# A decoder layer's MLP: up and gate products by seven block products in two passes, and the low parts of their weights on VectorE

## The reference

```python
qkv = _rms(x) @ w_qkv.T                     # x is LayerNorm(x) here
q, k, v = jnp.split(qkv, 3, axis=-1)
q, k = _rms(q), _rms(k)
w = jnp.exp(k)
y = sigmoid(q) * (cumsum(w * v) / (cumsum(w) + 1e-06))
u, g = jnp.split(y @ w_swiglu.T, 2, axis=-1)      # 2 x 2048 columns
x = x + u * silu(g) @ w_out.T
```

## Time and profile before

| | us |
|---|---|
| median of three runs | 1392.3 |
| the profiled execution: span | 1390.5 |
| TensorE busy | 1340.8 |
| VectorE busy | 819.9 |
| ScalarE busy | 606.6 |
| GpSimd busy | 513.0 |
| stage A, to the first `up` | 188.84 |
| the MLP, from there to the first transpose of the cross attention | 526.59 |

### The profile page before, as it was taken

One profiled execution on the slowest core, in us unless ns is written; L12 is line 12 of the kernel. 1 busy time (PEld: TensorE's weight loads), 2 busy tenths in 40 slices (PEclk: granted clock), 3 DMA queues, 4 the chain that ended last, 5 costly groups with the idle time before them and its releaser, 6 DMA issues.

```text
span 1390.5 us, 23678 instructions
## 1 busy us (share of the span) xinstructions
PE 1340.8 (96%) x8180; PEld 1068.0 (77%) x8180; DVE 819.9 (59%) x2085; ACT 606.6 (44%) x1135; POOL 513.0 (37%) x485
## 2 busy tenths in 40 slices
PE   8999999999999999999999999999988999999994
PEld 6788888888888888888886777777766877766762
DVE  5888865333333333333467787788786586666661
ACT  4444441111111111111126777777786324777772
POOL 4555542202020202020427554446453112655552
PEclk9999999999999999999999999999999999999997
DMA  6000002010110101010100000000011924566553
GB/s 257 1 0 0 0 30 107 0 46 5 42 38 8 45 0 45 0 46 1 49 12 17 21 21 21 21 5 17 6 47 46 374 81 159 92 106 105 95 98 46
DMA packets 20533, 73.41 MB, mean 53 GB/s; under 512 B 2320, under 2 KB 3344, under 8 KB 18000
## 3 DMA queue, kind: packets, MB, share of 16 engines
q1 hardware_dynamic: 10256, 46.93, 9.3%
q0 software_dynamic: 10176, 25.17, 9.2%
HBM read 52.95 MB, written 19.14 MB: 52 GB/s over the span
## 4 chain that ended last, share of the span: by engine, by line
PE 86%; DVE 6%; ACT 4%; issue 2%; DMA 1%; POOL 1%; POOLq 0%; DVEq 0%; SPq 0%; ACTq 0%
PE ps L782 21%; PE ps L784 21%; PE ps L783 21%; PE ps L1030 5%; PE ps L1215 5%; PE ps L1022 2%; DVE den L1641 2%; ACT cols L1434 2%; PE ps L1054 2%; PE ps L1122 2%; PE ps L1048 1%; ACT cols L1422 1%; PE ps L1185 1%; PE ps L1143 1%; PE ps L1019 1%
## 5 line engine op out<-in xcount | busy, mean ns | idle before, releaser
L782 PE MATMUL ps<-feat,wsplit 128*128 128x512 f32 (+1 forms) x672 | 247.1, 368 | 3.2 <-PE ps L784 2.1
L784 PE MATMUL ps<-feat,wsplit 128*128 128x512 f32 (+1 forms) x672 | 244.6, 364 | 0.0
L783 PE MATMUL ps<-feat,wsplit 128*128 128x512 f32 (+1 forms) x672 | 244.5, 364 | 0.0
L1291 ACT ACTIVATE sg<-ps 128x512 f32<-128x512 f32 x64 | 38.3, 598 | 369.1 <-PE ps L784 369.0
L1561 DVE TENSOR_TENSOR m_f<-ps,sg 128x512 f32<-128x512 f32 x64 | 44.2, 691 | 245.4 <-ACT sg L1291 245.4
L542 POOL CAST wsplit<-wraw 128x3072 fp32r<-128x3072 f32 x9 | 24.8, 2755 | 399.3 <-PEq L970 386.7
L1829 DVE CUSTOM_DVE_ANT_0 cols<-ps,msk 128x256 f32<-128x256 f32 (+1 forms) x512 | 146.2, 353 | 27.7 <-PE ps L1022 16.3
L782 PEld LDWEIGHTS ps<-feat,wsplit 128*128 128x128 f32 x672 | 126.7, 189 | 26.4 <-issue 6.6
L1422 ACT COPY cols<-ps 128x512 f32<-128x512 f32 x192 | 111.6, 581 | 77.7 <-PE ps L1030 77.7
L784 PEld LDWEIGHTS ps<-feat,wsplit 128*128 128x128 f32 x672 | 126.6, 188 | 19.9
L783 PEld LDWEIGHTS ps<-feat,wsplit 128*128 128x128 f32 x672 | 126.7, 189 | 19.7
(11 more groups left out here) (281 smaller groups left out, 3014.5 us busy)
## 6 DMA issues: line engine op xcount, KB each, us to landing
wraw<-weights SPq DMA_DIRECT2D x11, 1536.0 KB, 6.5
rawx<-weights SPq DMA_DIRECT2D x8, 1536.0 KB, 16.1
ctx_raw<-ctx_t SPq DMA_DIRECT2D x8, 512.0 KB, 4.6
h_rows<-hd POOLq DMA_DIRECT2D x16, 256.0 KB, 4.4
out<-acc SPq DMA_DIRECT2D x4, 1024.0 KB, 4.7
qkv_raw<-weights SPq DMA_DIRECT2D x6, 512.0 KB, 7.5
acc<-x SPq DMA_DIRECT2D x1, 3072.0 KB, 17.5
acc<-x SPq DMA_DIRECT2D x2, 512.0 KB, 7.0
```

The lines of the kernel that those rows point to most:

```text
L782: nc.tensor.matmul(out_, w_hi, m_hi, start=first, stop=False)
L783: nc.tensor.matmul(out_, w_lo, m_hi, start=False, stop=False)
L784: return nc.tensor.matmul(out_, w_hi, m_lo, start=False, stop=last)
```

## The change

Up and gate of a pair of token chunks are one product of a 2x2 block matrix of weights (rows: gate and up; columns: the two halves of K) by a 2x2 block matrix of y (the halves of K; two chunks of 512 tokens). The change makes it with seven block products in place of eight: sums of weight blocks (S1 to S4) and sums of y blocks (T1 to T4) are made first, and the seven products p1 to p7 are added up, in PSUM where one follows another in the same bank, and by copies (ScalarE) and additions (VectorE) elsewhere. A pass takes 1,024 tokens (batches 0 to 3, then 4 to 7) through all 8 groups, so there are 16 turns (`TURNS`), and all weights are loaded twice.

On TensorE, a product and its waits, `down`, and a turn:

```diff
+            def product(u, j, bank, w_op, y, y_op, first):
+                w = w_up[u % 2]
+                for k in range(HALF):
+                    out_ = ps[:, bank[j], :]
+                    w_hi, w_lo = w[:, j, 0, w_op, k, :], w[:, j, 1, w_op, k, :]
+                    y_hi, y_lo = y[:, y_op, 0, k, :], y[:, y_op, 1, k, :]
+                    nc.tensor.matmul(out_, w_hi, y_hi, start=first and k == 0, stop=False, skip_group_check=True)
+                    nc.tensor.matmul(out_, w_lo, y_hi, start=False, stop=False, skip_group_check=True)
+                    mm = nc.tensor.matmul(out_, w_hi, y_lo, start=False, stop=k == HALF - 1, skip_group_check=True)
+                return mm
...
+            def p1(u, j):
+                after(pe, mlp["silu2"], JB * (u - 1) + j + 1)
+                if u == 0 and j == 1:
+                    pe.wait_ge(a["w"], TILES)
+                pe.wait_ge(mlp["w_up"], JB * u + j + 1)
+                y_ready(u, 1)
+                product(u, j, BANK_X, A11, ya, B11, True).then_inc(mlp["P1"], 1)
...
+            def down(u, t):
+                chunk, o = t // 4, slice(t % 4 * P, (t % 4 + 1) * P)
+                pe.wait_ge(mlp["lo"], 2 * JB * u + JB * (chunk + 1))
+                pe.wait_ge(mlp["w_dn"], u + 1)
+                after(pe, mlp["acc"], PIECES * u + t - 1)
+                for j in range(JB):
+                    mm = three(pe, ps[:, BANK_D[t % 2], :], m_s[:, 0, j, chunk, o], m_s[:, 1, j, chunk, o],
+                               w_dn[u % 2][:, 0, j, :], w_dn[u % 2][:, 1, j, :], j == 0, j == JB - 1)
+                mm.then_inc(mlp["down"], 1)
...
+            for u in range(1, TURNS):
+                p1(u, 0)
+                p1(u, 1)
+                p2(u, 0)
+                p2(u, 1)
+                if u == 1:
+                    pe.wait_ge(a["y"], 2 * BATCH)
+                down(u - 1, 0)
+                p7(u, 0)
+                p7(u, 1)
+                down(u - 1, 1)
+                p6(u, 0)
+                p6(u, 1)
+                down(u - 1, 2)
+                down(u - 1, 3)
+                p5(u, 0)
+                p5(u, 1)
+                down(u - 1, 4)
+                p4(u, 0)
+                p4(u, 1)
+                down(u - 1, 5)
+                down(u - 1, 6)
+                p3(u, 0)
+                p3(u, 1)
+                down(u - 1, 7)
```

On VectorE, the weights' low parts (`low_plain`, `low_sums`), and where they and `first_rows` stand in a turn:

```diff
+            def low_of(v, j, ops, n):
+                dve.wait_ge(mlp["w_hi"], 4 * v + n)
+                to, raw = w_up[v % 2], w_up_raw[v % 2]
+                dve.wait_ge(mlp["ws"], v + 2)
+                return nc.vector.tensor_tensor(out=to[:, j, 1, ops, :, :].rearrange("p o k n -> p (o k n)"), in0=raw[:, j, 1, ops, :].rearrange("p o n -> p (o n)"),
+                                               in1=to[:, j, 0, ops, :, :].rearrange("p o k n -> p (o k n)"), op=ALU.subtract)
+            def low_plain(v):
+                for j in range(JB):
+                    low_of(v, j, slice(A11, A22 + 1), j + 1)
+            def low_sums(v, j):
+                low_of(v, j, slice(S1, S4 + 1), JB + j + 1).then_inc(mlp["w_up"], 1)
...
+            for u in range(1, TURNS):
+                gate_1(u, 0)
+                gate_1(u, 1)
+                sum_down(u - 1, 0)
...
+                if u + 1 == TURNS:
+                    first_rows()
+                sum_down(u - 1, 1)
...
+                sum_down(u - 1, 4)
+                up_1(u, 0)
+                up_1(u, 1)
+                hidden_1(u, 0)
+                hidden_1(u, 1)
+                sum_down(u - 1, 5)
+                if u + 1 < TURNS:
+                    low_plain(u + 1)
+                low(u, 0, 0)
+                low(u, 1, 0)
+                sum_down(u - 1, 6)
+                if u + 1 < TURNS:
+                    low_sums(u + 1, 0)
+                hidden_2(u, 0)
+                hidden_2(u, 1)
+                sum_down(u - 1, 7)
+                if u + 1 < TURNS:
+                    low_sums(u + 1, 1)
+                low(u, 0, 1)
```

On GpSimd, the sums of weights, the low part of the down weights, the second pass's sums of y, and (first lines) the first two of the ten pieces of y sums that stand behind the low parts of half batches (3,0) to (7,1) of stage A:

```diff
+                    if (b, tt) == (3, 0):
+                        y_sums(0, (T3, T1))
+                    if (b, tt) == (3, 1):
+                        y_sums(0, (T2, T4))
...
+            def weight_sums(to, of, a21, js):
+                s1 = own.mark(nc.gpsimd.tensor_tensor(out=to[:, js, 1, S1, :], in0=a21, in1=of(A22), op=ALU.add))
+                own.mark(nc.gpsimd.tensor_tensor(out=to[:, js, 1, S3, :], in0=of(A11), in1=a21, op=ALU.subtract))
+                own.wait(s1)
+                own.link(nc.gpsimd.tensor_tensor(out=to[:, js, 1, S2, :], in0=to[:, js, 1, S1, :], in1=of(A11), op=ALU.subtract))
+                nc.gpsimd.tensor_tensor(out=to[:, js, 1, S4, :], in0=of(A12), in1=to[:, js, 1, S2, :], op=ALU.subtract).then_inc(mlp["ws"], 1)
...
+            def split_dn(v):
+                pool.wait_ge(mlp["dn_hi"], v + 1)
+                nc.gpsimd.tensor_tensor(out=w_dn[v % 2][:, 1, :, :], in0=w_dn_raw[v % 2][:, 1, :, :], in1=w_dn[v % 2][:, 0, :, :], op=ALU.subtract).then_inc(mlp["w_dn"], 1)
...
+            def second_sums():
+                s_, n = a["T"], 2 * 4
+                pool.wait_ge(mlp["U2"], JB * MLP_GROUPS)
+                pool.wait_ge(a["y"], 2 * BATCH)
+                nc.gpsimd.tensor_tensor(out=y_whole(yt_raw, T3, 1), in0=y_chunk(1, 1), in1=y_chunk(1, 0), op=ALU.subtract).then_inc(s_, 1)
+                pool.wait_ge(s_, n + 1)
+                nc.gpsimd.tensor_tensor(out=y_whole(yt_raw, T2, 1), in0=y_whole(yt_raw, T3, 1), in1=y_chunk(0, 0), op=ALU.add).then_inc(s_, 1)
...
+            for u in range(TURNS):
+                if u + 1 < TURNS:
+                    split_up(u + 1)
+                split_dn(u)
+                if u + 1 == MLP_GROUPS:
+                    second_sums()
```

On ScalarE, the casts of the weights:

```diff
+            def up_hi(v):
+                act.wait_ge(raw_up, 32 * v)
+                for j in range(JB):
+                    nc.scalar.copy(w_up[v % 2][:, j, 0, A11:A22 + 1, :, :].rearrange("p o k n -> p (o k n)"),
+                                   w_up_raw[v % 2][:, j, 1, A11:A22 + 1, :].rearrange("p o n -> p (o n)")).then_inc(mlp["w_hi"], 1)
+                for j in range(JB):
+                    sums_hi(v, j, v + 2)
+            def dn_hi(v):
+                act.wait_ge(raw_dn, 16 * (v + 1))
+                nc.scalar.copy(w_dn[v % 2][:, 0, :, :], w_dn_raw[v % 2][:, 1, :, :]).then_inc(mlp["dn_hi"], 1)
```

More of the change, by code:

```diff
@@ L380, in decoder_layer @@
             w_hi="tiles of its hi", wv="tiles of w * v", wv_hi="tiles of its hi", split="tiles with w and w * v split",
-            w_hi_piece="pieces of w_qkv with hi", w_piece="pieces split", w2_hi="parts of the first MLP slot with hi", w2="parts split", shift="batches whose residual's scale and shift are made",
+            w_hi_piece="pieces of w_qkv with hi", w_piece="pieces split", shift="batches whose residual's scale and shift are made",
             w_sum="running sums of w, half batches", scan="those of w * v and exp(-q)^T too", wce="w's sums plus 1e-6",
-            den="denominators", rec="their reciprocals", y="outputs, half batches", yhi="their hi in feat", yT="their lo too",
+            den="denominators", rec="their reciprocals", y="outputs, half batches", yhi="operands made of them, their hi", yT="their lo too", T="sums of outputs", T_lo="the first pair's, split",
             pool="GpSimd's own small steps", dve="the vector engine's")
@@ L417, in decoder_layer @@
         mlp = signals(
-            "mlp_", up="up and gate in PSUM", silu="silu(gate)", m="silu(gate) * up", hi="its hi", lo="its lo",
-            down="sums in PSUM", acc="sums added to the residual")
+            "mlp_", P1="product 1 in PSUM", gate0="a copy of it", P2="product 2 in PSUM", P7="product 7 in PSUM", up0="a copy of it", gate1="first chunk's gate", silu1="its silu", U2="products 1 and 6", us="a copy of them",
+            U4="products 1, 6, 5 and 7", up2="second chunk's up", V="product 7 less product 4", up1="first chunk's up", X="second chunk's gate in PSUM", silu2="its silu",
+            m="silu(gate) * up", hi="their hi", lo="their lo", down="sums in PSUM", acc="sums added to the residual",
+            ws="slots with the weights' sums", w_hi="pieces of up weights with hi", w_up="hidden blocks with up weights split", dn_hi="slots with down weights' hi", w_dn="slots with down weights split")
         block = es.enter_context(nc.Block())
@@ L1003, in turned_unit @@
+            pe.wait_ge(mlp["silu2"], JB * TURNS)
+            for t in range(TPB):
+                turn_h(0, t, ps[:, 2 + t, :])
+            pe.wait_ge(slot_w, 1)
+            pe.wait_ge(c["ctx_s"], 1)
+            keys(ps[:, 0, :])
+            values(ps[:, 1, :])
+            for t in range(PIECES):
+                down(TURNS - 1, t)
+            pe.wait_ge(c["hT"], TPB)
+            for half in range(2):
+                queries(half, ps[:, 2 + half, :])
             def turned_unit(b, u):
```

873 lines of the change are left out of this document (522 added, 351 removed).

## The result

The changed kernel took 1438.1 us (median of 4 runs, 1435.7 to 1447.4) against 1392.2 before: a ratio of 1.034, with a 95% interval of 1.031 to 1.037. It is slower by 46 us, where 37 were forecast; the time lies in the stated range.

A forecast was written before the change was run, and what follows sets the result against it. TensorE was taken as the bound, busy 1340.8 of 1390.5 us, by matmul count and waits. Terms -43.5 + 31.9 + 9 + 25.3 + 4.1 + 13 - 3.0 = +36.8 gave 1429 us, range 1404 to 1454.

The forecast's parts named there:

- (a): TensorE in the MLP: 192 fewer matmuls at 0.2267 us each, -43.5 us.
- (b): Turn ends in the MLP: TensorE waits 2.28 us for VectorE's weight subtractions at 14 boundaries, +31.9 us.
- (c): Stage A: GpSimd's added pieces of y sums delay the scales and `ha`, +9 us, bounds 0 and 14.
- (d): First turn: waits of 13.2 us before and 8.7 us after it, 3.4 us for the clock, together +25.3 us.
- (e): Turn 7: GpSimd's y sums for the second pass hold two VectorE instructions, +4.1 us, bounds 0 and 6.
- (f): Turn 15: TensorE waits for a sum behind the first rows, which wait for their scale, +13 us.
- (g): MLP: the 3.0 us it lost before are replaced by the new waits, -3.0 us.
- Rival B: Turn ends: the weight subtractions are covered, VectorE being idle over 60% of the MLP; 1385 us, chance 0.11.
- Rival C: Stage A: GpSimd's new pieces don't reach TensorE, the start waits 7 us less; 1413 us, chance 0.14.
- rival E: Every turn: GpSimd's 2.41 us subtraction holds VectorE behind p4, 14 times, 34 us; 1463 us, chance 0.04.
- Rival D: Turn boundaries: two close waits cost a clock drop of 1.7 us at each of 14; 1453 us, chance 0.14.

The follow-up runs named there:

- run with all early: The changed kernel with all four weight subtractions of a turn moved earlier in VectorE's queue, turn 1's into turn 0: 1393.1 us, ratio 1.0005 to the kernel before.
- run with the scale first: The changed kernel with GpSimd making the first rows' scale ahead of the last down weights' low part and two stores in the last turn: 1432.0 us.
- run with p1 and p2 without the y sums: The changed kernel with p1 and p2 of turn 0 no longer waiting for the y sums' low parts; p6 and p7 do: 1436.3 us.

## Why the prediction was right

It was right in direction, in cause and within its range; the sum, 36.8, was 8.5 us short of the spans' difference, 45.3. By its steps, as the trace of the change shows them:

| step | forecast | measured, and from where |
|---|---|---|
| (a) 192 matmuls fewer | -43.5 | the matmuls of a turn without waits take 29.93 us (run with all early): as forecast |
| (b) 14 boundaries | +31.9 | 32.30 - 29.92 is 2.38, by 14: +33.3 |
| (c) stage A | +9 | TensorE's wait begins at 200.73, where `up` began at 188.84: +11.9 |
| (d) first wait | +13.2 | 15.43 |
| (d) wait at turn 1 | +8.7 | 13.58 |
| (d) two drops of the clock | +3.4 | 0.64 of the clock over 5.84 us and 0.60 over 5.85: +4.4 |
| (e) turn 7 | +4.1 | 36.03 - 32.30: +3.7 |
| (f) turn 15 | +13 | 12.37, and 0.72 of the clock over 5.76 us, 1.6: +14.0 |
| (g) idle time before | -3.0 | replaced, as forecast |
| stages after the MLP | 0 | -3.7: from the first scores on, 653.8 us where there were 657.5 |

That comes to 46.1, against 45.3. Nearly all steps were sized too small, by 13.4 us together; (e) was 0.4 too large, and the 3.7 us gained behind the MLP, which no step foresaw, hid part of the rest. That part of the nearness is luck.

(b) is the step that decides, and it was right to a tenth of a microsecond per turn: the chain was read off the order and priced from the rows of other lines, and its 10.44 us are what the trace of the boundary shows; the tenth is the slow start after a wait. The three runs that move the same four instructions confirm it from different sides: two earlier, two thirds of the wait gone; four earlier, none left; four on GpSimd, none left. Rival B was wrong only in that it took place for granted: VectorE did have the room, but not behind p4.

(c) was a quarter too small. The waits of 2.7 us at the transposes let the clock fall twice (0.94 and 0.93 of it over 27 and 26 us, 3.4 us), which the step did not count; the bounds held it. Batches with pieces became 2.2 to 4.3 us longer, where 2.3 were forecast (from reciprocal to reciprocal, 24.9 to 26.9 us where they took 22.5 to 22.7 before). Rival C fell with it: with four pieces moved behind q's scale, the wait ahead of turn 0 begins at 194.18 in place of 200.73.

(d) was mis-sized twice. The first wait was 2.2 us longer than forecast; this was not taken apart. At turn 1 it was 4.9 us longer. The forecast let GpSimd's subtraction of the down weights hold VectorE's hidden low part, which it did, but it missed what GpSimd does next. GpSimd, and VectorE beside it:

```profile
245.88 2.34 POOL L764 TENSOR_TENSOR w_dn<-w_dn_raw,w_dn 128x1024 fp32r<-128x1024 f32 x1 [24.78 <-ACT w_dn L1541]
248.31 1.58 POOL L742 TENSOR_TENSOR w_up_raw<-w_up_raw 128x512 f32<-128x512 f32 x1
...
251.52 1.97 POOL L745 TENSOR_TENSOR w_up_raw<-w_up_raw 128x512 f32<-128x512 f32 x1
```

```profile
246.35 4.09 DVE L2032 TENSOR_TENSOR m_s<-ups__92,m_s 128x512 fp32r<-128x512 f32 x2 [0.54 <-ACT m_s L1606]
250.36 7.28 DVE L2045 TENSOR_TENSOR w_up<-w_up_raw,w_up 128x768 fp32r<-128x768 f32 x4
```

GpSimd goes on at once with the weight sums for turn 2, and the two engines take turns: VectorE's four subtractions take 7.28 us in place of 4.1, and GpSimd's sums 1.58 to 1.97 in place of 1.27 to 1.30. Of the 4.9 us some 0.8 lie ahead of the end of GpSimd's subtraction, 1.0 in the hidden low part, which meets the first weight sum too, and the rest, over 3, in the three of VectorE's subtractions that p1 waits for. That is rival E's collision, in one turn instead of all.

(e) was right in place and size. In turn 7 the two products of `hidden_1` wait for GpSimd's sums of y: they take 4.57 us from 476.69 in place of 1.29, to 481.26, which is 0.55 us behind the end of GpSimd's last sum (from 477.86, 2.85 long). The boundary's chain starts that much later, and 0.5 us come on top where its last subtraction takes 1.71 in place of 1.22, beside a weight sum of GpSimd.

(f) was right in the change. The later expectation that taking the wait away gives all of it back was incomplete, as the run with the scale first showed.

Rival D, the clock at each boundary, did not come: the granted clock of the five turns is 1.00, with two waits of 0.55 and 1.31 in each.

Open: the 3.7 us gained behind the MLP. Before, a wait of 1.04 and one of 1.20 us close together lowered the clock behind the cross attention, to 0.72 over six microseconds, 1.7 us. In the change the second wait is 0.73 us and the clock behind it 1.00; in the run with all early it is 0.96 and the clock 1.00 too. That is some 2.2 of the 3.7 us. Why the wait became shorter was not tried, nor where the others come from.

## What to carry to other kernels

An instruction that is moved to a faster or idler engine takes the place that it gets in that engine's queue, and that place can cost more than the instruction: what has its inputs early belongs ahead of the wait for late ones, and a count of room on the engine does not tell. When a product count is cut, each wait that is added at a boundary has to be multiplied by the number of boundaries before the saved matmuls are counted as gain: here 2.38 us by 14 ate three quarters of 43.5. And after one wait is removed, look at what it had hidden: here a 7 us instruction on GpSimd that met VectorE only once TensorE was early.

## What was not expected of the hardware

- A wait of TensorE costs about 0.26 us more than its idle time in the trace (0.91 for 0.65 shown; in the change 2.38 for two that show 1.86), because of where a matmul's end is placed and how the first one after a wait starts.
- VectorE and GpSimd in streams of instructions with both operands in SBUF take turns: both slow down, VectorE's four from 4.1 to 7.28 us, GpSimd's 128x512 sum from 1.27 to as much as 1.97 at turn 1 and 2.27 behind turn 7.
- Waits of 2.7 us ahead of the transposes lowered the granted clock in two of three cases (0.94, 1.00 and 0.93 in the three batches), while a wait of 2.1 us before had not the earlier trace rows. Nor did the same wait lower it alike in two runs: 0.63 in the change and 0.52 in the run with p1 and p2 without the y sums, over the 6.3 us behind the wait at turn 1.
